# Constant rows written by VectorE, gate fills and count totals in other places, and the walk's layer norms normalised by GpSimd

## The reference

```
x = x + 0.5 * ffn(layernorm(x))      # top-2 of 8 experts, capacity cap = 1280 tokens
x = x + attn(layernorm(x))           # 16 heads of 16, causal
x = x + 0.5 * ffn(layernorm(x))

# ffn: probs = softmax(x @ gate_w.T); top-2 experts of each token
counts = bincount(a_e)               # tokens per expert over all 8192 tokens
keep = counts <= cap                 # an expert that is over its capacity gives nothing
```

## Time and profile before

| | us |
|---|---|
| time, median of 3 runs (lowest, highest) | 1428.04 (1427.39, 1428.27) |
| the profiled execution | 1428.08 |
| its span | 1426.2 |
| batches 1 to 6, each | 162.4 |

### The profile page before, as it was taken

The page is one execution under the profiler, slowest core; times in us unless marked ns, Lnnn a source line. Parts: engine busy times, 40 slices in busy tenths (PEclk is TensorE's granted clock), DMA queues, the critical chain, the costliest instruction groups (busy, mean ns, idle before and its releaser), DMA issues.

```text
span 1426.2 us, 24417 instructions
## 1 busy us (share of the span) xinstructions
PE 1271.6 (89%) x8352; PEld 548.5 (38%) x8352; DVE 1077.6 (76%) x3523; ACT 959.0 (67%) x1701; POOL 396.2 (28%) x510
## 2 busy tenths in 40 slices
PE   3479999999999999999999999999999999998883
PEld 1223333444344433444334433444334433433232
DVE  3079877878888788887888788877888788779544
ACT  1526777676777677676777677677776777666661
POOL 2032422233223322233222323232232323221110
PEclk9789999999999999999999999999999999999897
DMA  3366224254333424354332433354331343330000
GB/s 103 56 117 113 53 45 79 38 97 97 57 68 67 87 62 71 53 97 86 67 68 51 86 68 68 67 97 85 67 68 35 55 85 68 56 68 30 1 15 19
DMA packets 56343, 95.16 MB, mean 67 GB/s; under 512 B 8208, under 2 KB 49808, under 8 KB 50064
## 3 DMA queue, kind: packets, MB, share of 16 engines
q1 hardware_dynamic: 54176, 92.30, 34.5%
q10 hardware_dynamic: 2032, 1.19, 0.3%
HBM read 59.91 MB, written 33.55 MB: 66 GB/s over the span
## 4 chain that ended last, share of the span: by engine, by line
PE 61%; DVE 15%; ACT 14%; issue 6%; POOL 2%; DVEq 2%; POOLq 0%; ACTq 0%
PE o_bank L1190 15%; PE s L1171 13%; PE st L1158 11%; PE misc L1112 9%; DVE s L948 5%; ACT q_stack L781 5%; ACT probs L794 4%; PE misc L1107 4%; PE misc L1135 4%; DVE max_full L952 3%; PE misc L489 3%; ACT qk L754 2%; ACT parts L754 2%; POOL probs L664 1%; DVE o_tok L1029 1%
## 5 line engine op out<-in xcount | busy, mean ns | idle before, releaser
L794 ACT ACTIVATE probs<-st 128x512 f32<-128x512 f32 (+1 forms) x1216 | 634.0, 583 | 219.1 <-PE st L1158 125.8
L948 DVE CUSTOM_DVE_ANT_0 s<-s,causal 128x128 f32<-128x128 f32 (+3 forms) x1024 | 494.6, 503 | 177.4 <-PE s L1171 174.0
L1171 PE MATMUL s<-k_stack,q_stack 96*128 96x512 bf16 (+3 forms) x1536 | 493.6, 333 | 23.3 <-DVE max_diag L948 9.7
L1158 PE MATMUL st<-q_stack,k_stack 108*128 108x512 bf16 (+3 forms) x1536 | 486.6, 330 | 26.3 <-ACT probs L794 24.0
L952 DVE TENSOR_REDUCE max_full<-s 128x1 f32<-128x512 f32 x512 | 350.0, 684 | 34.2 <-PE s L1171 32.8
L1190 PE MATMUL o_bank<-probs,v_aug 128*17 128x512 f32 (+3 forms) x3072 | 324.8, 495 | 10.6 <-POOL probs L664 9.3
L664 POOL TENSOR_SCALAR_AFFINE_SELECT probs<-probs 128x512 f32<-128x512 f32 x256 | 163.6, 644 | 526.5 <-ACT probs L794 526.3
L1171 PEld LDWEIGHTS s<-k_stack,q_stack 96*128 96x128 bf16 x1536 | 149.5, 98 | 383.1 <-DVE max_diag L948 175.3
L1158 PEld LDWEIGHTS st<-q_stack,k_stack 108*128 108x128 bf16 x1536 | 150.2, 98 | 149.1 <-ACT probs L794 61.3
L676 POOL TENSOR_TENSOR qk<-qk,parts 128x512 f32<-128x512 f32 x64 | 74.2, 1160 | 336.7 <-ACT parts L754 336.7
L781 ACT ACTIVATE q_stack<-misc 12x2048 bf16<-12x2048 f32 x64 | 119.7, 1870 | 37.7 <-PE misc L1141 36.3
(11 more groups left out here) (87 smaller groups left out, 820.3 us busy)
## 6 DMA issues: line engine op xcount, KB each, us to landing
part_dram<-parts SPq DMA_DIRECT2D x128, 192.0 KB, 2.8
k_stack<-part_dram SPq DMA_DIRECT2D x192, 128.0 KB, 6.9
q_stack<-part_dram SPq DMA_DIRECT2D x32, 384.0 KB, 5.0
x_all<-x SPq DMA_DIRECT2D x16, 512.0 KB, 10.5
q_stack<-part_dram SPq DMA_DIRECT2D x32, 256.0 KB, 7.4
out<-x_all SPq DMA_DIRECT2D x7, 1024.0 KB, 10.6
q_stack<-part_dram SPq DMA_DIRECT2D x32, 128.0 KB, 8.8
w_qk<-wqk_t ACTq DMA_DIRECT2D x1, 512.0 KB, 5.4
```

What stands on the lines that cost most here:

```text
L794: nc.scalar.activation(probs[:, g % 2, h - part:h + 1, 0:width], st_bank[i % 3][:, 0:share * width] .rearrange("p (h c) -> p h c", c=width ...
L948: nc.vector.tensor_tensor_reduce(out=bank, in0=bank, in1=causal[:, CW - width:CW], scale=1.0, scalar=-BIG, op0=ALU.add, op1=ALU.max, accum ...
L1158: score = nc.tensor.matmul(st_bank[i % 3][:, part * width:(part + 1) * width], k_stack[0:KROWS + MROWS, hg, h, jb * P:(jb + 1) * P], q_sta ...
L1171: nc.tensor.matmul(s_bank[u % 3][:, 0:width], q_stack[0:KROWS, hm, h, ib * P:(ib + 1) * P], k_stack[0:KROWS, hm, h, j0:j0 + width], start= ...
```

## The change

Constant rows: `ones` moves from ScalarE's handler to VectorE's, where it is a `tensor_copy` of the same rows. In the prologue the two projections of head group 1 move out of the loop of maxima to places between the `v` fills.

Gate fills: `lg0` and `lt0`, at units 7 and 12 in steps 2 and 3, go to 12 and 17 in step 2 and 12 and 28 in step 3.

Totals: the counts are added by a matmul with a column of ones (of `v_aug`) instead of `partition_all_reduce`. In batch 7, step 2, it is a fill of `misc` at unit 7, `total0`, which VectorE reads and frees; the entry `decide0` at unit 10 goes. After the walk it is one matmul more.

Layer norms: the `lnnorm` entries of "next" and "last" in the batches are GpSimd's. There are 112 such instructions, 16 in each of batches 1 to 6. The prologue's, "this" and "pair" stay on VectorE. `lnaggr` on VectorE now waits for the normalisations before it.

```diff
-    "end": (24, 26, 29, 32, 35), "top2": 17, "before": (7, 12), "xload": 0, "top0": (2, 4), "count0": 2,
-    "decide0": 10,
+    "end": (24, 26, 29, 32, 35), "top2": 17, "before": ((12, 17), (12, 28)), "xload": 0, "top0": (2, 4), "count0": 2,
+    "total0": 7,
...
-    plan += [(3, "use", "v", j) for j in range(4)] + [(3, "ones", hq) for hq in range(NG)]
+    plan += [(3, "use", "v", j) for j in range(2)] + project(1, 0) + [(3, "use", "v", j) for j in range(2, 4)]
+    plan += project(1, 1) + [(3, "ones", hq) for hq in range(NG)]
...
-    halves = [(hq, c) for hq in range(1, NG) for c in range(2)]
+    halves = [(hq, c) for hq in range(2, NG) for c in range(2)]
...
-        def vector_normalise(t, tile, dst=xn):
-            return nc.vector.tensor_scalar(dst[:, t, :], x_tiles(tile, 1)[:, 0, :], mean_var[:, t, 0:1],
-                                           rstd[:, t:t + 1], ALU.subtract, ALU.mult)
+        def normalise(engine, t, tile):
+            return engine.tensor_scalar(xn[:, t, :], x_tiles(tile, 1)[:, 0, :], mean_var[:, t, 0:1],
+                                        rstd[:, t:t + 1], ALU.subtract, ALU.mult)
+
+        def normalised_by_pool(b, what):
+
+            return b >= 0 and what in ("next", "last")
...
-            def all_counts(layer):
-                eng.wait_ge(counted, layer + 1)
-                nc.gpsimd.partition_all_reduce(total[:, :], counts[:, :], P, ADD_REDUCE).then_inc(totalled, 1)
...
+                elif kind == "lnnorm" and normalised_by_pool(b, a[0]):
+                    what, c, t = a
+                    if t == 0:
+                        eng.wait_ge(sig.rstd_ready, n("lnaggr"))
+                        eng.wait_ge(sig.misc_full, n("use"))
+                    normalise(nc.gpsimd, t, lin(b, TB, BATCH[what] * TB + c * CT + t)).then_inc(sig.xn_ready, 1)
...
-                elif kind == "count0":
-                    all_counts(0)
...
-                elif kind == "ones":
-                    if sig.spec:
-                        hq = a[0]
-                        eng.wait_ge(max_rows_ready, MPARTS)
-                        rows = nc.scalar.activation(k_stack[KROWS:P, hq, :, :],
-                                                    row_of_head[:, :, :].to_broadcast([32, HG, S]), ACT.Copy)
...
-            def decide(layer):
+            def decide(layer, taken):
 
                 vec = nc.vector
-                eng.wait_ge(totalled, layer + 1)
-                vec.tensor_scalar(kept[:, 0, :], total[:, :], float(CAP), None, ALU.is_le)
+                vec.tensor_scalar(kept[:, 0, :], misc[:, 0:E], float(CAP), None, ALU.is_le).then_inc(taken, 1)
...
-                    else:
+                    elif not normalised_by_pool(b, what):
...
                 elif kind == "lnaggr":
+                    if n("lnnorm") > 0:
+                        eng.wait_ge(sig.xn_ready, n("lnnorm"))
                     vector_aggregate(eng).then_inc(sig.stats_ready, 1)
...
+                elif kind == "ones":
+                    if sig.spec:
+                        hq = a[0]
+                        eng.wait_ge(max_rows_ready, MPARTS)
+                        rows = nc.vector.tensor_copy(k_stack[KROWS:P, hq, :, :],
+                                                     row_of_head[:, :, :].to_broadcast([32, HG, S]))
...
-                elif kind == "decide0":
-                    decide(0)
+                elif kind == "use" and a[0] == "total0":
+                    eng.wait_ge(sig.misc_full, n("use", 1))
+                    decide(0, sig.misc_free)
...
+            def total_counts():
+
+                return nc.tensor.matmul(misc[:, 0:E], v_aug[:, 0, 0, HD:VW].to_broadcast([P, P]), counts[:, :],
+                                        start=True, stop=True)
...
+                elif what == "total0":
+                    eng.wait_ge(counted, 1)
+                    last = total_counts()
...
+            eng.wait_ge(counted, 2)
+            total_counts().then_inc(totalled, 1)
             if_kept(eng, 1, lambda: moe_tensor(1))
```

More of the change, by code:

```diff
@@ L26 @@
 AX = mybir.AxisListType
-ADD_REDUCE = bass.bass_isa.ReduceOp.add
 B, S, D = 8, 1024, 256
@@ L181, in step_plan @@
     if hg >= 2 and nxt and spec:
-        put(PLACE["before"][0], ("use", "lg0", hg - 2))
-        put(PLACE["before"][1], ("use", "lt0", hg - 2))
+        for u, what in zip(PLACE["before"][hg - 2], ("lg0", "lt0")):
+            put(u, ("use", what, hg - 2))
     if hg == 1 and spec:
@@ L191, in step_plan @@
             put(PLACE["count0"], ("count0",))
-            put(PLACE["decide0"], ("decide0",))
+            put(PLACE["total0"], ("use", "total0"))
     if hg == NG - 1 and not nxt:
@@ L376, in program @@
         late_counts = sb("late_counts", [P, E])
-        total = sb("total", [P, E])
         kept = sb("kept", [P, 1, E])
@@ L425, in program @@
         totalled = sem("totalled")
+        total_taken = sem("total_taken")
         flag_ready = sem("flag_ready")
@@ L699, in _ @@
             run(eng, attention, moe_pool, idle, lambda: None)
-            all_counts(1)
             if_kept(eng, 1, lambda: moe_pool(1))
@@ L737, in evict @@
             def evict(sig, b, n, hg, what, *a):
-                if what in ("otr", "wo"):
+                if what in ("otr", "wo", "total0"):
                     return
@@ L817, in handle @@
                     eng.wait_ge(bias_scaled, 1)
-                elif kind == "ones":
-                    if sig.spec:
-                        hq = a[0]
-                        eng.wait_ge(max_rows_ready, MPARTS)
-                        rows = nc.scalar.activation(k_stack[KROWS:P, hq, :, :],
-                                                    row_of_head[:, :, :].to_broadcast([32, HG, S]), ACT.Copy)
-                        if hq == NG - 1:
-                            rows.then_inc(max_rows_ready, 1)
             def idle():
@@ L913, in chunk @@
                     for t in range(CT):
-                        last = vector_normalise(t, c * CT + t)
+                        last = normalise(nc.vector, t, c * CT + t)
                     last.then_inc(baton[layer], 1)
@@ L989, in handle @@
                             eng.wait_ge(sig.rstd_ready, n("lnaggr"))
-                        vector_normalise(t, tile).then_inc(sig.xn_ready, 1)
+                        normalise(nc.vector, t, tile).then_inc(sig.xn_ready, 1)
                 elif kind == "lnaggr" and a[0] == "pair":
+                    eng.wait_ge(sig.xn_ready, n("lnnorm"))
                     vector_aggregate(eng, (2 * a[1], 2 * a[1] + 1)).then_inc(sig.stats_ready, 1)
@@ L1005, in handle @@
                                                 ALU.mult).then_inc(bias_scaled, 1)
+                elif kind == "ones":
[4 more added lines that the diff above has]
+                                                     row_of_head[:, :, :].to_broadcast([32, HG, S]))
+                        if hq == NG - 1:
+                            rows.then_inc(max_rows_ready, 1)
                 elif kind == "top0":
@@ L1062, in _ @@
             nc.vector.tensor_tensor(counts[:, :], counts[:, :], late_counts[:, :], ALU.add).then_inc(counted, 1)
-            decide(1)
+            eng.wait_ge(totalled, 1)
+            decide(1, total_taken)
             if_kept(eng, 1, lambda: moe_vector(1))
```

## The result

The changed kernel takes 1503.7 us (median of 4 runs, 1502.6 to 1506.48) against 1428.15 (4 runs, 1427.39 to 1428.34): the ratio is 1.0533, 95% interval 1.0515 to 1.0551. It is slower by 5.3%, on the side that was forecast but far above the range of 1421 to 1449. The profiled execution took 1502.68 us with a span of 1500.8. Two single executions further on, 2400.65 us of the kernel before and 5993.65 us of the kernel with the tiles four units earlier, stand apart from all the others and are in no ratio.

The account below looks back on a forecast made before the run. TensorE was taken to bound the kernel, the question being whether tiles arrive in time: 1428.08 + 16.2 (batches 1 to 6) + 0.5 (batch 0) - 1 (constant rows) - 5.5 (batch 7) + 0 = 1438.3 us; range 1421 to 1449.

Parts of the forecast that it names:

- What bounds the kernel: Whole kernel: TensorE busy 1271.6 of 1426.2 us; work taken off VectorE or ScalarE is worth only what TensorE waits for.
- The queue of GpSimd: Middle batch: two tiles queue behind the select, which waits for exponentials; net +1.4, +0.2, +1.1 us, together +2.7 a batch.
- the three transposes named: PE L489 waiting for POOL at units 38, 19 and 18 (steps 0, 2, 3): 1.4, 0.7 and 1.3 us.
- Price of a tile: One 256-column normalisation on GpSimd: 0.50 us, bounds 0.40 to 0.75, from affine select and two-input addition; 0.41 on VectorE.
- The clock: Batch 7, step 2: PE's half-clock stretch after a wait gives back some 1.1 us; no clock loss charged for new waits.
- Gate fills: Steps 2 and 3: moving lg0 saves 0.5 us each; moving lt0 costs nothing in step 2, 0.3 in step 3.
- Constant rows: Prologue: four VectorE copies at 2.3 us each, maxima +0.6, following loop -1.2 to -2; net -1 us, bounds -7 to +8.
- Totals: Matmul for partition reduction: -4.1 us in batch 7 step 2, 0 at the end; batch 7 in all -5.5.
- an exchange of libraries: Batch 7, step 2: GpSimd's issue gaps of 6.0 and 7.65 us around the reduction read as an instruction library exchanged twice.
- the slow one (1455): Rival, everything at the slow price: copies at L952's price (+8 us), tiles at 0.75 (+9); 1455 us, chance 0.12.
- The forecast of 165.1 for a middle batch: Middle batch in the profile after: 165.1 us, against 162.40 before; at or under 162.4 would prove the prediction wrong.

Follow-up runs that it names:

- where the tiles came nearly in time: Changed kernel with every batch norm on GpSimd four units earlier, the transposes that waited left in place: 1426.14 us, ratio 0.9979.
- split tiles: Changed kernel with each normalisation of the batches split, 32 columns on GpSimd and 224 on VectorE: 1453.04 us, ratio 1.0166.

## Why the prediction was wrong

- *What bounds the kernel*: right. Work taken off VectorE gained nothing by itself (128 us busy a batch instead of 131, and 164.3 a batch even where the tiles came nearly in time, for 161.5 with them on VectorE), and the question was whether the tiles come in time.
- *The queue of GpSimd*: right, to the units. Waits arose at exactly the three transposes named, by the mechanism named, and at the forecast's price they are 3.1 us a batch for 3.4.
- *Price of a tile*: the step that failed. I took 0.50 us with an upper bound of 0.75; it is 1.222. The bounds were not bounds: the select is another operation, and the two-input addition, my upper end, has one arithmetic step where this has two. The nearest row in kind was one I passed by. The rstd's `TENSOR_SCALAR` on GpSimd also has two steps, but it has 4 elements and so shows only the fixed part. No row had the slope of this operation, so the end above should have been open. The prediction's estimate of 0.61 us from the Trainium skill (GPSIMD Engine Reference, 3.1 Elementwise — side-by-side cycle accounting) is below the measured 1.22 as well. The page names its 1.8 cycles an element as a best case at 1.2 GHz; the measured 3.3 ns an element would be about 4 such cycles. With 1.22 the sum of waits is 7.8 us a batch instead of 3.4, and of the 13.5 us between 162.4 and 175.9 (the mean of batches 2 to 6) this explains 4.4 beyond the forecast.
- *The clock*: a term that the sum did not have, 6.0 us a batch, larger than what the waits were short by. The rows for it were there: I used the window at 0.50 behind the wait in batch 7 to credit a gain of 1.1 us where a wait went, and did not debit the same where three new waits came. Behind waits of 2.2 to 2.8 us the clock fell in all three places. At the forecast's price it fell in two of the three in most batches and cost 3.3 us a batch, as much as the waits themselves, so that the kernel took 1453.04 us: with the right price and nothing for the clock the forecast would still have been too low. That a wait costs more than its length was in the trace; not to apply it both ways was the error.
- *Gate fills*: -0.5 in each of two steps was forecast, less 0.3 for lt0; measured -0.87 in batch 3 (162.39 to 161.52). Right, with the cause found by exclusion.
- *Constant rows*: a copy takes 2.25 us alone and up to 2.76 in the mean beside work of GpSimd, for the 2.3 assumed. Of the two readings that the prediction set side by side, it is the slower. Net nothing alone (ratio 0.9997) for -1 forecast: right within its bounds. In company of the totals' change the prologue is shorter by some 3 us (100.7 for 103.7), but with the same prologue batch 0 began anywhere from 98.6 to 102.9 in seven profiles: at 98.6 to 100.7 in the four whose first fill of `v` took 1.99 us, and at 101.5 to 102.9 in the three where it took 3.78, as it did in the 103.7. So how much of the 3 us belongs to this part is open.
- *Totals*: step 2 of batch 7 gained 4.4 in the kernel that has only this part, for 4.1. In the changed kernel two new waits for tiles (2.12 in step 2, 5.23 in step 3, in the trace of after) hide it, so that batch 7 and the end are +1.7 instead of -5.5. The step that failed is the start of the program. I read the 6.0 and 7.65 us on GpSimd as an exchange of libraries, since nothing else there waited for issue so long. That was false: 12.92 us of the same kind stand before its first select. They go with the partition reduction too, and PE's first matmul came 8.7 us earlier. That it is libraries that are exchanged was argued and is not shown by a run; that the reduction in the program is the cause is shown.
- *The rivals*: the slow one (1455) had the right sign of the surprise, and too little of it, since it took its price from the same false bound. The forecast of 165.1 for a middle batch is not met even at its own price: the split tiles show 168.3 in the mean, 166.4 at best.

Put together: forecast 1438; +4.4 a batch of longer waits and +6.0 a batch of slow clock are 62 of the +64 in batches 1 to 6; +3.5 in batch 0; +7.2 in batch 7, where the tiles hide the totals' gain; -10.4 in the prologue. These come to 64.3, and 1438.3 + 64.3 is the profiled execution's 1502.7 to 0.1. The surprise in the prologue hid 10 us of what the tiles cost beyond the forecast.

## What to carry to other kernels

An operation's price on another engine is bounded only by a row of that operation there; where the trace has none, leave the upper end open, and ask at which price the mechanism turns. Where work goes to an engine with an in-order queue, list what stands in front of it there and what that waits for: the engine was idle two thirds of the time, and still late. A new wait of TensorE is to be charged with its length and with the slower matmuls after it, and the rows where an old wait ends show how much (here behind every wait of 2.2 us or more, and behind those of 1.2 to 1.3 in most batches); a transfer of work that is placed early enough, as in the run with norms four units earlier, costs a fifth of the same work placed late.

## What the runs showed of the hardware

- The two-step `tensor_scalar` on fp32 takes 0.37 us and 3.3 ns a column on GpSimd, 1.22 us for 128x256, three times VectorE's 0.41. Its 32 columns took 0.487 us and its 128 columns 0.795.
- With a partition reduction in the program GpSimd stood still for 12.9 us before its first select and for 6.0 and 7.65 us around the reduction in batch 7; without it all three are gone.
- GpSimd and VectorE can slow each other. Beside the bf16 copies of 4096 elements a two-input operation of GpSimd took 3.25 instead of 1.15 us. In batch 7, step 3 of the changed kernel a two-input operation of VectorE took 1.09 instead of 0.59 beside GpSimd's select and the tile behind it, and its neighbours of two inputs took 0.59 to 0.79. Two tiles there took 2.87 instead of 2.43 (below). In batch 3 VectorE shows nothing of this: no group of VectorE's operations takes over 0.1 us more in sum than with the tiles on VectorE.

```profile
1437.60 1.09 DVE L852 SCALAR_TENSOR_TENSOR x_t<-x_t,logits 128x416 f32<-128x416 f32 x1
...
1438.24 2.87 POOL L465 TENSOR_SCALAR xn<-x_all,mean_var,rstd 128x256 f32<-128x256 f32 x2
...
1441.26 1.09 PE L493 MATMUL misc<-ident,xn 128*128 128x128 f32 x4 [5.23 <-POOL xn L465]
```

It stays open what decides whether the clock falls. With split tiles it fell behind the waits of 1.27 us in step 0 and of 1.19 in step 3 in five batches of six each, and in the sixth not, so at this size the length of the wait alone does not settle it; behind 0.65 us it never fell, and behind 2.2 to 2.8 us always.
